# Preamble of a fused convolution and LoRA kernel: taps and bias loaded as whole rows, three unread products, the first pair's merges and chunks in another order, B's high part stored by itself

## The chip, the cores and the metric

One core of a Trainium2 chip runs the kernel. The metric is the device time of one execution in microseconds; less is better.

## The reference, cut to what matters

x has 64 samples of 64 channels by 1024 positions. First comes a grouped convolution along the positions (4 groups, 9 taps, padding 4), plus a context per sample and channel and a bias:

```
out = conv(x, weight, groups=4) + (c @ c_weight.T)[:, :, None] + bias[None, :, None]
```

Its result, seen as 8 batches of 512 rows by 1024, goes through a dense layer with LoRA: a kernel W of 1024 by 1024 and a bias, a pair A, B per batch (gate, 8 by 16, mixes 16 of them; rank 32) and a shared pair:

```
y @ W + bias + (y @ A_eff[b].T) @ B_eff[b].T + (y @ A_s.T) @ B_s.T
```

and x is added. Everything is float32.

## The kernel before, in words

**Tiling.** A batch b has 8 samples; a half h of it holds two of the four groups, and each group t of a half is one tile of 128 rows, for which TensorE computes `main[t]`. A pair of tiles (b, h) is a *unit*; the sixteen units run one after the other. For speed in float32, each operand is split into a high part (`x_hi`, `y_hi`, `w_hi`) and a low part, the rest (`x_lo`, ...), and three products of the parts are summed. ScalarE makes high parts, GpSimd (and VectorE for some of the first) the low ones by a subtraction; VectorE takes convolution results out of PSUM (`y_add`) and transposes them (`y_stage`). From the second batch on the convolution has a fast form with three products per tile (`fast`, L890 to L892), which also needs differences of x: `xd` and, in place, `x_tr` (`x_diff`, L649 and L653), turned into `xd_hi`, `x_hi` (L505, L507) and `xd_lo`, `x_lo` (L358, L360).

**The preamble.** Before the loop everything is prepared and the first pair of tiles is computed beside it. The taps `w_pad` are spread out to `z_all` (L599), transposed by TensorE (L827), and split into `t_hi`, `t_lo`. The context is `cond` times `cond_w` plus a bias column `cb_col`; TensorE brings the 64 words `cbias` to the partitions with a product by a selection matrix `sel` (L834), and multiplies at L842. `gmix` is gate, spread by TensorE (L955). With it, TensorE mixes A (`mix_a`, L914; VectorE turns the result in `a_turn`, L687, into `a_eff`) and B (`mix_b`, L927; `b_turn`, L692, into `be_raw`). The shared pair is merged into W: `merge(m)` (L902) multiplies half m of B_s A_s, `w_add(m)` (L683, VectorE) adds it to `w_raw`, `w_high(k)` (ScalarE, L511) and `w_low(k)` (GpSimd, L383) split chunk k of 8. `chunk(k)` then multiplies the first pair by chunk k: eight products by `w_hi`, then four by `w_lo`. The first four convolution tiles are `convolve(0, 0, i)` and `y_tile(0, 0, i)`; the order of everything is written out by hand for each engine, and each engine works its own list strictly in order, with semaphores between them.

The first half of x is transposed by VectorE in four pieces (L612), then split (L470, L676 on VectorE for t = 0, L334 on GpSimd for t = 1); the second half of x follows in the same way.

**B for the later batches.** `be_raw` is split into `be_hi` (L550) and `be_lo` (L398); the first batch's rows go to `b_cur` with six transfers (L266, semaphore `b_first`), and all of both parts to HBM, `b_scratch`, with eight (L274, semaphore `be_out`), after both parts are complete. The memory of `be_hi` is used again by `xd_hi` and `xd_lo`: so `x_high(2, ...)` on ScalarE waits for `b_first` and for all of `be_out`. SyncE (SP) issues nearly all transfers, in the order of its list; ScalarE's queue issues the taps, `cond_nat`, `cw_nat` and `cbias`.

**The steady part.** From the second unit on, `unit(b, h)` on TensorE has 48 products of 512 columns per tile with W (L936: 8 chunks, 3 products of parts, 2 halves of the columns), the product with A (L949), the low rank part (L941) and two fast convolutions for the next unit. Output goes from `res` to HBM by SyncE.

Of the kernel before, what the change touches and what calls it, by code (L numbers as in the profile page):

```python
# [5 lines left out]
F32 = mybir.dt.float32  # L6
F32R = mybir.dt.float32r
ALU = mybir.AluOpType
ACT = mybir.ActivationFunctionType
# [41 lines left out]
def adaln_ffn(nc, x, x_rows, cond, cond_bias, conv_w, cond_w, gate, kern, bias,  # L51
# [10 lines left out]
    with ctx:  # L62
# [9 lines left out]
        def early(*specs):  # L72
# [32 lines left out]
        (w_pad, cond_nat, cw_nat, cond_t, cw_rep, cbias, cb_col, sel, gate_nat, gate_rep, diag) = early(  # L105
            ("w_pad", [C, CG, PAD + TAPS + PAD], F32), ("cond_nat", [NS, CD], F32), ("cw_nat", [C, CD], F32),
            ("cond_t", [CD, NS], F32), ("cw_rep", [P, G, J, CG], F32), ("cbias", [CG, G], F32), ("cb_col", [P, G], F32), ("sel", [CG, J, CG], F32),
# [14 lines left out]
        ident_ready, halo_zero, pad_zero = sem("ident_ready"), sem("halo_zero"), sem("pad_zero")  # L122
# [7 lines left out]
        ctx_mm, ctx_done, sel_done = sem("ctx_mm"), sem("ctx_done"), sem("sel_done")  # L130
# [6 lines left out]
        be_hid, be_lod, be_out, b_first = sem("be_hid"), sem("be_lod"), sem("be_out"), sem("b_first")  # L137
# [78 lines left out]
        def _(sp):  # L216
            load_first(sp, 0)
# [106 lines left out]
        def _(pool):  # L324
# [4 lines left out]
            pool.wait_ge(ident_ready, 2)  # L329
            nc.gpsimd.tensor_copy(sel[:, :, :], ident[0:CG, 0:CG].unsqueeze(1).broadcast_to([CG, J, CG])).then_inc(sel_done, 1)  # L330
# [116 lines left out]
        def _(act):  # L447
            act.dma_start(w_pad[:, :, PAD:PAD + TAPS], conv_w).then_inc(cw_in, 16)
            act.dma_start(cond_nat[:, :], cond).then_inc(cond_in, 16)
            act.dma_start(cw_nat[:, :], cond_w).then_inc(cond_in, 16)  # L450
            with nc.allow_non_contiguous_dma(reason="sixty-four words"):
                act.dma_start(cbias[:, :], cond_bias.rearrange("(g c) -> c g", g=G)).then_inc(cbias_in, 16)
# [9 lines left out]
            nc.scalar.activation(cb_col[:, :], rank[:, 128:128 + G], ACT.Copy).then_inc(cond_cp, 1)  # L462
# [10 lines left out]
            act.wait_ge(tlo_done, 2)  # L473
            nc.scalar.activation(t01_raw[:, :, :, :].rearrange("p g s c -> p s g c"),
                                 main[0][:, 512:1024].rearrange("p (s g c) -> p s g c", s=J, g=G), ACT.Copy).then_inc(t01_copied, 1)
# [8 lines left out]
            nc.scalar.activation(bias_hi[:, :], bias_nat[:, :], ACT.Copy).then_inc(bias_split, 1)  # L484

# [47 lines left out]
            w_high(3)  # L533
# [52 lines left out]
        def _(dve):  # L586
            nc.vector.memset(w_pad[:, :, 0:PAD], 0.0).then_inc(pad_zero, 1)
            nc.vector.memset(w_pad[:, :, PAD + TAPS:], 0.0).then_inc(pad_zero, 1)
# [7 lines left out]
            dve.wait_ge(pad_zero, 2)  # L596
            dve.wait_ge(cw_in, 16)
            wide = PAD + TAPS + PAD
# [108 lines left out]
            dve.wait_ge(bs_in, 48)  # L707
            nc.vector.transpose(bs_t[0:STACK, :].rearrange("r (p o) -> r o p", p=R), bs_rep[0:STACK, :, :]).then_inc(bs_turned, 1)
# [395 lines left out]
```

## Time and profile before

| | |
|---|---|
| median of 3 runs | 509.15 us (508.51 to 509.65) |
| the profiled execution | 507.94 us |
| its span in the trace | 506.1 us |
| TensorE busy (matmuls) | 488.4 us, 96% |
| weight loads of TensorE | 403.1 us, 80% |
| VectorE, ScalarE, GpSimd busy | 332.9, 166.7, 272.7 us |
| chain that ended last: TensorE, DMA, VectorE | 90%, 3%, 2% |
| transfers | 65.04 MB, mean 129 GB/s |

Busy time of TensorE is the time in which a matmul is under way; matmuls overlap, so it doesn't say how fast they go. Times below are microseconds from the start of the span. A row of a timeline gives the start, the duration, the engine (PE is TensorE, PEld its weight loads, DVE VectorE, ACT ScalarE, POOL GpSimd, SPq and ACTq the queues that issue transfers), the line, the operation, its output and inputs, shapes, the number of instructions merged, and in brackets how long the engine had been idle and what ended that.

### The profile page before, as it was taken

How to read it: one execution, taken by the hardware profiler on the slowest of the kernel's cores; microseconds unless marked ns; L12 is line 12 of the kernel's file. 1: busy time of each engine (PE TensorE's matmuls, PEld its weight loads, DVE VectorE, ACT ScalarE, POOL GpSimd, SP SyncE). 2: the span in 40 equal slices, each digit the busy share in tenths (PEclk: the TensorE clock that was granted, in tenths of full speed). 3: DMA queues.
4: the chain of work that ended last, by engine and by line, in shares of the span. 5: the costliest groups of instructions: out<-in, count | busy, mean ns of one | idle time of the engine just before them, and what ended most of it. 6: DMA issues, size and time to landing. Idle time of an engine off the chain costs nothing.

```text
span 506.1 us, 6740 instructions
## 1 busy us (share of the span) xinstructions
PE 488.4 (96%) x2394; PEld 403.1 (80%) x2394; DVE 332.9 (66%) x384; ACT 166.7 (33%) x210; POOL 272.7 (54%) x157
## 2 busy tenths in 40 slices
PE   2999998999999999999999999999999999999995
PEld 2777886788888888888888888888888888888884
DVE  4786585996938497575939397575948488473411
ACT  2566313341525123331524224331433234331100
POOL 0789943792847439272756529282665619382200
PEclk9999999899999999999999999999999999999998
DMA  8953526751724326241634326241633313241303
GB/s 216 416 217 138 188 69 172 243 199 67 240 94 114 83 70 239 51 128 41 230 102 111 86 52 241 57 124 55 214 117 100 97 29 83 66 122 63 99 27 83
DMA packets 19029, 65.04 MB, mean 129 GB/s; under 512 B 2728, under 2 KB 3368, under 8 KB 18376
## 3 DMA queue, kind: packets, MB, share of 16 engines
q1 hardware_dynamic: 17736, 64.77, 41.3%
q10 hardware_dynamic: 1280, 0.10, 0.2%
q8 instruction: 8, 0.13, 0.1%
q14 instruction: 5, 0.04, 0.0%
HBM read 45.59 MB, written 18.87 MB: 127 GB/s over the span
## 4 chain that ended last, share of the span: by engine, by line
PE 90%; DMA 3%; DVE 2%; POOL 1%; ACT 1%; SPq 1%; issue 0%; ACTq 0%; DVEq 0%
PE main L936 65%; PE rank L949 5%; PE main L941 3%; PE conv L890 3%; PE conv L892 3%; PE conv L891 3%; PE conv L866 2%; DMA cbias<-in_fside_S 2%; PE main L914 1%; PE spare L892 1%; PE spare L891 1%; PE spare L890 1%; SPq L274 1%; DMA b_scratch<-be_lo 1%; PE conv L927 1%; POOL x_lo L360 1%
## 5 line engine op out<-in xcount | busy, mean ns | idle before, releaser
L936 PE MATMUL main<-w_hi,y_hi 128*128 128x512 f32 x512 | 160.1, 391 | 0.0
L936 PE MATMUL main<-w_hi,y_lo 128*128 128x512 f32 x512 | 159.0, 389 | 0.0
L936 PE MATMUL main<-w_lo,y_hi 128*128 128x512 f32 x512 | 158.2, 390 | 0.0
L936 PEld LDWEIGHTS main<-w_lo,y_hi 128*128 128x128 f32 x512 | 96.4, 188 | 20.6
L378 POOL TENSOR_TENSOR y_lo<-y_stage,y_hi 128x512 fp32r<-128x512 f32 x56 | 94.0, 1701 | 34.0 <-ACT y_hi L494 34.0
L936 PEld LDWEIGHTS main<-w_hi,y_lo 128*128 128x128 f32 x512 | 96.1, 188 | 20.3
L936 PEld LDWEIGHTS main<-w_hi,y_hi 128*128 128x128 f32 x512 | 95.3, 188 | 19.4
L358 POOL TENSOR_TENSOR xd_lo<-xd,xd_hi 128x512 fp32r<-128x512 f32 x28 | 39.3, 1404 | 104.2 <-ACT xd_hi L505 104.2
L360 POOL TENSOR_TENSOR x_lo<-x_tr,x_hi 128x1024 fp32r<-128x1024 f32 x28 | 82.6, 2948 | 16.5 <-ACT x_hi L507 16.5
L507 ACT ACTIVATE x_hi<-x_tr 128x1024 fp32r<-128x1024 f32 x28 | 57.7, 2061 | 30.0 <-DVE x_tr L653 30.0
L494 ACT ACTIVATE y_hi<-y_stage 128x512 fp32r<-128x512 f32 x56 | 35.5, 634 | 90.2 <-DVE y_stage L671 90.2
L671 DVE STREAM_TRANSPOSE y_stage<-y_add 128x512 f32<-128x512 f32 x56 | 62.9, 1163 | 0.0
L761 DVE TENSOR_TENSOR ax_sum<-rank,ax_sum 32x256 f32<-32x256 f32 x16 | 6.6, 412 | 71.4 <-ACT ax_sum L518 71.4
L769 DVE TENSOR_TENSOR res<-main,res 128x1024 f32<-128x1024 f32 x31 | 37.5, 1210 | 22.9 <-PE main L941 22.9
L505 ACT ACTIVATE xd_hi<-xd 128x512 fp32r<-128x512 f32 x28 | 17.8, 634 | 99.0 <-DVE xd L649 87.7
L653 DVE TENSOR_TENSOR x_tr<-x_tr 128x512 f32<-128x512 f32 x28 | 46.1, 1646 | 1.0
L649 DVE TENSOR_TENSOR xd<-x_tr 128x512 f32<-128x512 f32 x28 | 39.9, 1423 | 4.4 <-POOL xd_lo L358 4.4
L612 DVE STREAM_TRANSPOSE x_tr<-x_in 128x512 f32<-128x512 f32 (+1 forms) x64 | 39.3, 678 | 1.8 <-DMA x_in<-in_x_rows 1.6
L662 DVE TENSOR_TENSOR y_add<-conv,ctx_all 128x512 f32<-128x512 f32 x28 | 19.1, 684 | 22.8 <-PE conv L892 22.8
L949 PE MATMUL rank<-y_hi,a_cur 128*64 128x256 f32 x128 | 29.9, 277 | 0.0
L949 PE MATMUL rank<-y_lo,a_cur 128*64 128x256 f32 x128 | 29.9, 277 | 0.0
L518 ACT ACTIVATE ax_sum<-rank 32x256 f32<-32x256 f32 x16 | 6.0, 373 | 60.4 <-PE rank L949 60.4
(105 smaller groups left out, 489.1 us busy)
## 6 DMA issues: line engine op xcount, KB each, us to landing
res<-in_x SPq DMA_DIRECT2D x32, 512.0 KB
out<-res SPq DMA_DIRECT2D x31, 512.0 KB
x_in<-in_x_rows SPq DMA_DIRECT2D x7, 2048.0 KB, 12.8
w_raw<-in_L_ffn_kernel SPq DMA_DIRECT2D x4, 1024.0 KB, 17.8
b_cur<-b_scratch SPq DMA_DIRECT2D x21, 128.0 KB, 3.1
la<-in_L_ffn_lora_A SPq DMA_DIRECT2D x4, 512.0 KB, 8.1
lb<-in_L_ffn_lora_B SPq DMA_DIRECT2D x1, 2048.0 KB, 8.1
x_in<-in_x_rows SPq DMA_DIRECT2D x1, 1048.0 KB, 7.7
```

The costliest lines, as they stand in the source:

```text
L358: nc.gpsimd.tensor_tensor(xd_lo[:, t], xd[:, :, :], xd_hi[:, t].bitcast(F32), ALU.subtract).then_inc(xlo_done, 1)
L360: nc.gpsimd.tensor_tensor(x_lo[:, t, :, 0:NP], x_raw(2 * h + t, 0, NP), x_hi[:, t, :, 0:NP].bitcast(F32), ALU.subtract).then_inc(xlo_done, 1)
L378: nc.gpsimd.tensor_tensor(y_parity(y_lo, h, t, e), y_staged(e), y_parity(y_hi, h, t, e).bitcast(F32), ALU.subtract).then_inc(ylo_done, 1)
L494: nc.scalar.activation(y_parity(y_hi, h, t, e), y_staged(e), ACT.Copy).then_inc(yhi_done, 1)
L507: nc.scalar.activation(x_hi[:, t, :, 0:NP], x_raw(2 * h + t, 0, NP), ACT.Copy).then_inc(xhi_done, 1)
L612: nc.vector.transpose(x_tr[:, m0:m1, :, :].rearrange("p m n g -> p m (n g)"), blocks).then_inc(xt_done, 1)
L649: nc.vector.tensor_tensor(xd[:, :, :], x_block(0, 1, g), x_block(1, 0, g), ALU.subtract).then_inc(xd_done, 1)
L653: nc.vector.tensor_tensor(x_block(0, 0, g), x_block(0, 0, g), x_block(1, 0, g), ALU.subtract).then_inc(xd_done, 1)
L671: nc.vector.transpose(y_stage[:, e, :].rearrange("p (a l n c) -> p a n l c", a=2, l=2, n=SB), y_add[:, e, :].rearrange("p (a m n) -> p a n ...
L769: nc.vector.tensor_tensor(res[:, g, :], main[g % 2][:, :], res[:, g, :], ALU.add).then_inc(main_free, 1)
L936: mm(main[t][:, n * 512:(n + 1) * 512], lhs, rhs[:, k, n * 512:(n + 1) * 512], start=k == 0 and first, stop=False)
L949: last = mm(rank[0:2 * R, 0:2 * P], lhs, y[h][:, :, k, :], start=k == 0 and y is y_hi, stop=k == KC - 1 and y is y_lo)
```

## The change

Six things change, all in the preamble.

1. The taps are loaded as 64 whole rows (`w_nat`, 576 bytes each) and VectorE copies them into `w_pad`, in place of a transfer of 1024 pieces of 36 bytes.
2. The bias of the context is loaded as one row of 64 words, first on SyncE's queue. GpSimd repeats it (`bias_rep`), and four products of one row by one word (`ones`) bring it to `spare`; ScalarE copies it to `cb_col`. The matrix `sel` and its product are gone.
3. `fill(n)`: n products of `ident` with itself, 512 columns, into `main[1]`, which nobody reads. Two before the taps' transposes, one before the gate's product.
4. The first pair's work stands in another order: on TensorE `mix_a(2)` and `mix_a(3)` move forward, merges 4 to 11 move behind the chunks one step further; VectorE turns A before the second `y_tile`, makes `gmix` before it turns `bs_t`, and takes `w_add(6)` and `w_add(7)` after `y_tile(0, 0, 2)`; ScalarE and GpSimd exchange some `w_high`/`w_low` and `y`/`x` operations; the copy of `t01_raw` moves behind the split of the shared pair.
5. The four stores of `be_hi` are issued when `be_hi` is complete, with a semaphore of their own, `be_out[0]`; those of `be_lo` follow with `be_out[1]`.
6. `x_high(2, ...)` waits for `be_out[0]` and for the last `be_lod`, not for the stores of `be_lo`.

```
 sync:
+            sp.dma_start(cbias[:, :], cond_bias.rearrange("(a c) -> a c", a=1)).then_inc(cbias_in, 16)
             load_first(sp, 0)
...
-            sp.wait_ge(be_hid, RQ)
-            sp.wait_ge(be_lod, RQ)
-            for i, part in enumerate((be_hi, be_lo)):
+            for i, (part, split) in enumerate(((be_hi, be_hid), (be_lo, be_lod))):
+                sp.wait_ge(split, RQ)
                 for oh in range(2):
                     for bq in range(2):
...
-                                     part[row:row + R, :, :].bitcast(F32)).then_inc(be_out, 16)
+                                     part[row:row + R, :, :].bitcast(F32)).then_inc(be_out[i], 16)
             sp.wait_ge(b_first, 96)
-            sp.wait_ge(be_out, 128)
+            sp.wait_ge(be_out[0], 64)
+            sp.wait_ge(be_out[1], 64)
 gpsimd:
-            pool.wait_ge(ident_ready, 2)
-            nc.gpsimd.tensor_copy(sel[:, :, :], ident[0:CG, 0:CG].unsqueeze(1).broadcast_to([CG, J, CG])).then_inc(sel_done, 1)
+            nc.gpsimd.memset(ones[:, :], 1.0).then_inc(biasrep_done, 1)
+            pool.wait_ge(cbias_in, 16)
+            nc.gpsimd.tensor_copy(bias_rep[:, :, :, :], cbias[:, :].rearrange("a (g c) -> a g c", g=G)
+                                  .unsqueeze(2).broadcast_to([1, G, J, CG])).then_inc(biasrep_done, 1)
...
             w_low(2)
             x_first_low(1)
+            y_low_first(2)
             w_low(3)
-            y_low_first(2)
+            y_low_first(3)
             x_low_second(0)
-            y_low_first(3)
             w_low(4)
 scalar:
-            act.dma_start(w_pad[:, :, PAD:PAD + TAPS], conv_w).then_inc(cw_in, 16)
+            act.dma_start(w_nat[:, :], conv_w.rearrange("o c k -> o (c k)")).then_inc(cw_in, 16)
...
-                act.dma_start(cbias[:, :], cond_bias.rearrange("(g c) -> c g", g=G)).then_inc(cbias_in, 16)
...
-            nc.scalar.activation(cb_col[:, :], rank[:, 128:128 + G], ACT.Copy).then_inc(cond_cp, 1)
+            act.wait_ge(bias_mm, 1)
+            nc.scalar.activation(cb_col[:, :], spare[:, 64:64 + G], ACT.Copy).then_inc(cond_cp, 1)
...
-                    act.wait_ge(be_out, 128)
+                    act.wait_ge(be_out[0], 64)
+                    act.wait_ge(be_lod, RQ)
...
             x_first_high(1)
-            w_high(3)
             act.wait_ge(a_done, RQ)
...
             y_high_first(0, 2, FIRST)
+            w_high(3)
             x_high_second(0)
+            y_high_first(0, 3, FIRST)
             w_high(4)
-            y_high_first(0, 3, FIRST)
+            x_high_second(1)
             w_high(5)
-            x_high_second(1)
 vector:
+            nc.vector.tensor_copy(w_pad[:, :, PAD:PAD + TAPS], w_nat[:, :].rearrange("o (c k) -> o c k", k=TAPS)).then_inc(pad_done, 1)
+            dve.wait_ge(pad_done, 3)
...
             y_tile(0, 0, 0, FIRST, first=True)
+            a_turn(0)
             y_tile(0, 0, 1, FIRST, first=True)
-            a_turn(0)
+            a_turn(1)
...
-            a_turn(1)
+            a_turn(2)
             w_add(0)
             w_add(1)
-            a_turn(2)
+            a_turn(3)
             w_add(2)
             w_add(3)
-            a_turn(3)
...
+            x_first_low(1)
+            y_tile(0, 0, 2, FIRST, first=True)
             w_add(6)
             w_add(7)
-            x_first_low(1)
-            y_tile(0, 0, 2, FIRST, first=True)
-            w_add(8)
-            w_add(9)
             y_tile(0, 0, 3, FIRST, first=True)
-            w_add(10)
-            w_add(11)
+            for m in range(8, 12):
+                w_add(m)
 tensor:
+            def fill(n):
+                for _ in range(n):
+                    mm(main[1][:, 0:512], ident[:, :], ident[:, :].unsqueeze(1).broadcast_to([P, 4, P]), start=True, stop=True)
             pe.wait_ge(ident_ready, 2)
+            fill(2)
...
+            pe.wait_ge(biasrep_done, 2)
+            for g in range(G):
+                last = mm(spare[:, 64 + g:65 + g], bias_rep[:, g, :, :].rearrange("a j c -> a (j c)"), ones[:, :], start=True, stop=True)
+            last.then_inc(bias_mm, 1)
...
+            fill(1)
             pe.wait_ge(gate_cp, 1)
...
             mix_a(0)
             mix_a(1)
+            mix_a(2)
             merge(0)
             merge(1)
-            mix_a(2)
+            mix_a(3)
             merge(2)
             merge(3)
-            mix_a(3)
-            merge(4)
-            merge(5)
...
             chunk(0)
+            merge(4)
+            merge(5)
+            chunk(1)
+            convolve(0, 0, 2, FIRST, first=True)
             merge(6)
             merge(7)
-            chunk(1)
-            convolve(0, 0, 2, FIRST, first=True)
+            chunk(2)
+            convolve(0, 0, 3, FIRST, first=True)
             merge(8)
             merge(9)
-            chunk(2)
-            convolve(0, 0, 3, FIRST, first=True)
+            chunk(3)
             merge(10)
             merge(11)
-            chunk(3)
             mix_b(0)
```

## Rows read from the trace of the kernel before

**Rows 1.** Windows of 100 to 500 us, their sum by engine.

```profile
sum 400.00, PE 400.00 PEld 333.09 DVE 261.15 ACT 124.55 POOL 208.18; mean PE 44.44 PEld 37.01 DVE 29.02 ACT 13.84 POOL 23.13
```

**Rows 2.** Timeline of the first 25 us, all engines.

```profile
5.67 1.22 DVE L599 COPY z_all<-w_pad 64x2048 f32<-64x2048 f32 x1 [3.78 <-DMA w_pad<-in_L_cond_weight]
...
7.04 1.94 PE L827 MATMUL main<-ident,z_all 64*128 64x64 f32 x16 [7.04 <-DVE z_all L599]
...
8.54 2.56 DVE L612 STREAM_TRANSPOSE x_tr<-x_in 128x544 f32<-128x544 f32 x4 [1.64 <-DMA x_in<-in_x_rows]
...
12.93 2.10 ACT L470 ACTIVATE x_hi<-x_tr 128x528 fp32r<-128x528 f32 x2
12.94 1.94 PE L842 MATMUL rank<-cond_t,cw_rep 128*128 128x64 f32 x8 [0.89 <-ACT cb_col L462]
14.06 1.08 DVE L676 TENSOR_TENSOR x_lo<-x_tr,x_hi 128x528 fp32r<-128x528 f32 x1 [1.79 <-ACT x_hi L470]
...
15.39 2.08 DVE L708 STREAM_TRANSPOSE bs_t<-bs_rep 96x1024 f32<-96x1024 f32 x1
...
18.37 0.69 DVE L631 TENSOR_TENSOR y_add<-conv,ctx_all 128x512 f32<-128x512 f32 x1 [0.85 <-PE conv L866]
...
24.82 0.68 DVE L683 TENSOR_TENSOR w_raw<-rank,w_raw 128x512 f32<-128x512 f32 x1
```

**Rows 3.** Chain that ended last, before 100 us: start, duration, what.

```profile
15.40 4.44 PE conv L866 x24
...
44.90 1.87 PE conv L927 x8
...
47.44 2.74 PE main L936 x12
...
55.47 2.84 PE conv L866 x24
...
77.79 4.84 DMA b_scratch<-be_lo
```

**Rows 4.** Waits of TensorE before 100 us: total, times, longest.

```profile
PE conv L890 <- POOL x_lo L360: 2.5, 1, 2.5
```

**Rows 5.** Windows, 90 to 100 us: engines, granted clock, DMA share, GB/s.

```profile
90.00:100.00 10.00, 10.00 (x38) 8.02 (x37) 9.76 (x9) 3.98 (x4) 6.86 (x5) 0.83 0.77 253
```

**Rows 6.** Timeline of 78 to 97 us, all engines.

```profile
78.30 1.07 DVE L649 TENSOR_TENSOR xd<-x_tr 128x512 f32<-128x512 f32 x1
...
82.79 0.63 ACT L505 ACTIVATE xd_hi<-xd 128x512 fp32r<-128x512 f32 x1 [11.38 <-DMA b_scratch<-be_lo]
...
85.43 3.28 POOL L360 TENSOR_TENSOR x_lo<-x_tr,x_hi 128x1024 fp32r<-128x1024 f32 x1 [0.63 <-ACT x_hi L507]
...
93.27 2.96 POOL L360 TENSOR_TENSOR x_lo<-x_tr,x_hi 128x1024 fp32r<-128x1024 f32 x1 [3.14 <-ACT x_hi L507]
```

**Rows 7.** DMA issues before 100 us: queue, count, KB each, us to landing.

```profile
x_in<-in_x_rows SPq DMA_DIRECT2D x1, 1048.0 KB, 7.7
...
w_pad<-in_L_cond_weight ACTq DMA_DIRECT2D x1, 36.0 KB, 4.8
...
cw_nat<-in_L_cond_c_weight ACTq DMA_DIRECT2D x1, 32.0 KB, 8.0
```

**Rows 8.** DMA issues between 71.5 and 72 us.

```profile
b_scratch<-be_hi SPq DMA_DIRECT2D x1, 256.0 KB, 2.7
```

**Rows 9.** GpSimd's groups of instructions, 32.9 to 46 us: busy, mean ns.

```profile
L383 POOL TENSOR_TENSOR w_lo<-w_raw,w_hi 128x1024 fp32r<-128x1024 f32 x3 | 7.3, 2418 | 1.3 <-ACT w_hi L511 1.3
L352 POOL TENSOR_TENSOR x_lo<-x_tr,x_hi 128x1040 fp32r<-128x1040 f32 x1 | 3.0, 3005 | 0.5 <-ACT x_hi L525 0.5
L366 POOL TENSOR_TENSOR y_lo<-y_stage,y_hi 128x512 fp32r<-128x512 f32 x2 | 2.6, 1306 | 0.0
```

**Rows 10.** Timeline of 34 to 46 us, VectorE and GpSimd.

```profile
34.19 2.08 DVE L676 TENSOR_TENSOR x_lo<-x_tr,x_hi 128x512 fp32r<-128x512 f32 x1
...
45.99 4.76 POOL L383 TENSOR_TENSOR w_lo<-w_raw,w_hi 128x1024 fp32r<-128x1024 f32 x2
```

More of the change, by code:

```diff
@@ L104, in adaln_ffn @@
         y_add, y_stage = sb("y_add", [P, 2, 512]), sb("y_stage", [P, 2, 512])
-        (w_pad, cond_nat, cw_nat, cond_t, cw_rep, cbias, cb_col, sel, gate_nat, gate_rep, diag) = early(
+        (w_pad, cond_nat, cw_nat, cond_t, cw_rep, cbias, cb_col, bias_rep, ones, w_nat, gate_nat, gate_rep, diag) = early(
             ("w_pad", [C, CG, PAD + TAPS + PAD], F32), ("cond_nat", [NS, CD], F32), ("cw_nat", [C, CD], F32),
-            ("cond_t", [CD, NS], F32), ("cw_rep", [P, G, J, CG], F32), ("cbias", [CG, G], F32), ("cb_col", [P, G], F32), ("sel", [CG, J, CG], F32),
+            ("cond_t", [CD, NS], F32), ("cw_rep", [P, G, J, CG], F32), ("cbias", [1, C], F32), ("cb_col", [P, G], F32),
+            ("bias_rep", [1, G, J, CG], F32), ("ones", [1, 1], F32), ("w_nat", [C, CG * TAPS], F32),
             ("gate_nat", [NB, NL], F32),
@@ L120, in adaln_ffn @@
         rank = ps("rank", [P, 512])
-        ident_ready, halo_zero, pad_zero = sem("ident_ready"), sem("halo_zero"), sem("pad_zero")
+        ident_ready, halo_zero, pad_done = sem("ident_ready"), sem("halo_zero"), sem("pad_done")
         cw_in, cond_in, cbias_in, gate_in = sem("cw_in"), sem("cond_in"), sem("cbias_in"), sem("gate_in")
@@ L129, in adaln_ffn @@
         cond_tr, cond_cp, cwrep_done = sem("cond_tr"), sem("cond_cp"), sem("cwrep_done")
-        ctx_mm, ctx_done, sel_done = sem("ctx_mm"), sem("ctx_done"), sem("sel_done")
+        ctx_mm, ctx_done, bias_mm, biasrep_done = sem("ctx_mm"), sem("ctx_done"), sem("bias_mm"), sem("biasrep_done")
         gate_cp, gate_tr, diag_done, gmix_done = sem("gate_cp"), sem("gate_tr"), sem("diag_done"), sem("gmix_done")
@@ L136, in adaln_ffn @@
         a_mm, a_done, b_mm, b_turned = sem("a_mm"), sem("a_done"), sem("b_mm"), sem("b_turned")
-        be_hid, be_lod, be_out, b_first = sem("be_hid"), sem("be_lod"), sem("be_out"), sem("b_first")
+        be_hid, be_lod, b_first = sem("be_hid"), sem("be_lod"), sem("b_first")
+        be_out = [sem(f"be_out{i}") for i in range(2)]
         x0_hi, x0_lo, x0_pool, y0_lo = sem("x0_hi"), sem("x0_lo"), sem("x0_pool"), sem("y0_lo")
@@ L447, in _ @@
         def _(act):
-            act.dma_start(w_pad[:, :, PAD:PAD + TAPS], conv_w).then_inc(cw_in, 16)
+            act.dma_start(w_nat[:, :], conv_w.rearrange("o c k -> o (c k)")).then_inc(cw_in, 16)
             act.dma_start(cond_nat[:, :], cond).then_inc(cond_in, 16)
             act.dma_start(cw_nat[:, :], cond_w).then_inc(cond_in, 16)
-            with nc.allow_non_contiguous_dma(reason="sixty-four words"):
-                act.dma_start(cbias[:, :], cond_bias.rearrange("(g c) -> c g", g=G)).then_inc(cbias_in, 16)
             for w in range(2):
@@ L484, in _ @@
             nc.scalar.activation(bias_hi[:, :], bias_nat[:, :], ACT.Copy).then_inc(bias_split, 1)
+            act.wait_ge(tlo_done, 2)
+            nc.scalar.activation(t01_raw[:, :, :, :].rearrange("p g s c -> p s g c"),
+                                 main[0][:, 512:1024].rearrange("p (s g c) -> p s g c", s=J, g=G), ACT.Copy).then_inc(t01_copied, 1)
             def y_high_first(u, i, order):
@@ L586, in _ @@
         def _(dve):
-            nc.vector.memset(w_pad[:, :, 0:PAD], 0.0).then_inc(pad_zero, 1)
-            nc.vector.memset(w_pad[:, :, PAD + TAPS:], 0.0).then_inc(pad_zero, 1)
+            nc.vector.memset(w_pad[:, :, 0:PAD], 0.0).then_inc(pad_done, 1)
+            nc.vector.memset(w_pad[:, :, PAD + TAPS:], 0.0).then_inc(pad_done, 1)
             nc.vector.memset(x_in[:, :, 0:HALO], 0.0).then_inc(halo_zero, 1)
@@ L706, in _ @@
                                     cb_col[:, :].unsqueeze(2).broadcast_to([P, G, NS]), ALU.add).then_inc(ctx_done, 1)
-            dve.wait_ge(bs_in, 48)
-            nc.vector.transpose(bs_t[0:STACK, :].rearrange("r (p o) -> r o p", p=R), bs_rep[0:STACK, :, :]).then_inc(bs_turned, 1)
             dve.wait_ge(diag_done, 1)
@@ L712, in _ @@
                                     spare[:, 0:NB].unsqueeze(2).broadcast_to([P, NB, R8]), ALU.mult).then_inc(gmix_done, 1)
+            dve.wait_ge(bs_in, 48)
+            nc.vector.transpose(bs_t[0:STACK, :].rearrange("r (p o) -> r o p", p=R), bs_rep[0:STACK, :, :]).then_inc(bs_turned, 1)
             dve.wait_ge(ctx_done, 1)
             y_tile(0, 0, 0, FIRST, first=True)
+            a_turn(0)
             y_tile(0, 0, 1, FIRST, first=True)
-            a_turn(0)
+            a_turn(1)
             dve.wait_ge(t01_copied, 1)
@@ L830, in _ @@
                 last.then_inc(t_tr, 1)
-            pe.wait_ge(cbias_in, 16)
-            pe.wait_ge(sel_done, 1)
-            mm(rank[:, 128:128 + G], sel[:, :, :].rearrange("a j c -> a (j c)"), cbias[:, :],
-               start=True, stop=True)
             pe.wait_ge(cond_in, 32)
```

4 lines of the change are left out of this document (removed).

## The prediction

> **What bounds the kernel now.** I read the stretches of the span first. Between 100 and 500 us TensorE is busy for all 400 us at the full granted clock [rows 1], and the table of waits has no wait of TensorE after 88.8 us. So four fifths of the kernel is a TensorE stream that the change leaves alone: what it saves or loses before 100 us arrives at the end unchanged, and nothing else counts.
>
> Then the waits and the timeline before 100 us. TensorE starts at 7.04 us, when the spread-out taps are there [rows 2]; it is held twice between 9 and 13 us; its first convolutions (24 products) take 4.44 us, where the same work later takes 2.84 us [rows 3]: they start at the 1.2 GHz level, and the spacing of the products halves near 18.2 us, 5.2 us after the stream of work without a pause began at 12.94 us [rows 2]. (The granted-clock column says 1.00 here; the durations say otherwise, and I go by them.) From 15.3 to 86.1 us TensorE hardly pauses. Then it waits 2.5 us for GpSimd's x_lo [rows 4], and afterwards the granted clock of 90 to 100 us is 0.83 on average [rows 5]: the clock fell to 1.2 GHz behind the pause, which cost 0.17 x 10 = 1.7 us more.
>
> The chain of waits says why x_lo was late: the last store of B's low part, issued at 77.79 us, lands 4.84 us later [rows 3], and ScalarE's xd_hi sat 11.38 us until that [rows 6], since its buffer lies where be_hi lay. The data of xd_hi, VectorE's first difference, was there at 79.37 us.
>
> **Part by part: the taps and the bias.** The taps now come as 64 rows of 576 bytes instead of 1024 pieces of 36 bytes. Before: issue at 0.75 us, landing 4.8 us later [rows 7]. The quickest landing of a larger transfer in this trace took 2.7 us (256 KB) [rows 8]; I take that: 3.45 us. VectorE's new copy of 64x144 isn't in the trace; between nothing and the 1.22 us of z_all [rows 2], near 0.2 us by its size. z_all then ends at 4.95 us, TensorE starts at 5.05 (2.0 earlier) and ends its 16 transposes at 7.0. With no gain in the landing all of this stays at 7.0 and 9.0.
>
> The context's weights landed 8.0 us after their issue, at 10.15 us [rows 7], behind the 1024 pieces on the same queue. I take them as there by 7.0 us (2.7 us after issue would be 4.9; at worst 10.15 as before). The bias as one row on SyncE's queue replaces 64 single words on ScalarE's. It pushes the load of x by one issue, about 0.7 us. x landed 7.7 us after 0.74 [rows 7]; less the load of the small pieces, plus the 0.7 us, it lies between 6.7 and 9.2 us; I take 7.6. The chunk transposes [rows 2] then run to 10.15 us.
>
> The four new bias products on TensorE are like the context's eight entries (four products, 1.94 us, [rows 2]), and before there was one product of 0.58 us. They end at 7.0 + 0.5 (transposes of the context) + 1.94 = 9.45 us; ScalarE turns over cond_t and cw_rep beside them, copies the bias by 9.7 and starts x_hi at 10.2 us (before 12.93 [rows 2]). Context products 9.75 to about 11.1 us. **The fills**: two of them lie in time when TensorE has nothing else (1.5 to 3.4 us) and cost nothing; the third is an fp32 product of 512 columns, 1.87/4 = 0.47 us by the four of L927 [rows 3], twice that at 1.2 GHz, and it is on the path. The gate product 0.3 us, so the convolutions begin at 11.9 us. TensorE works nearly without a pause from 5.05 us; if the clock rises as long after this as before (5.2 us), it is up at 10.3 and the convolutions take 2.84 us: until 14.75 instead of 19.8 us.
>
> At the small pieces the trace shows 4.8 us for 36 KB and 2.7 us for 256 KB [rows 7, 8]. The Trainium skill (DMA: Bandwidth & Descriptors, Specifications) wants at least 512 bytes a transfer for the full rate, which 576 bytes meets and 36 doesn't; the trace agrees in direction. By the rule alone the gain would be the whole excess, the 2.1 us that I took; by the row, without it, nothing between 0 and 2.1 is excluded.
>
> **VectorE sets the next date.** x_lo (1.08 us, [rows 2]) ends at 12.5, context and gmix by 13.3, and bs_t of 2.08 us at 15.4: y_add starts there instead of at 18.37 us [rows 2]. From it to the end of the second sum of W were 7.1 us before, 0.3 of that idle; the new order puts one more turn of A (0.7 us) in: 7.6 us, so 23.0 us instead of 25.5 [rows 2]. The turn of A that now stands ahead of the second y_tile needs mix_a(0), which TensorE ends at 14.75 + 1.9 = 16.65, and VectorE is ready for it at 17.2: just no wait. W's first low part is done at 26.55 us, 2.5 earlier.
>
> **The interleaving gives most of it back.** TensorE now computes chunk 0 (2.74 us, [rows 3]) before merges 4 and 5, and must wait for that low part: chunk 0 and merges end near 27.9 us. VectorE's sums 4 and 5, the chunk transposes, x_hi and x_lo follow one another, and the third convolution ends at 34.2 us instead of 36.8, with about 2 us of waits of TensorE around it. w_add 6 and 7 are now behind y_tile 2, so w_hi(3) comes at 37.4 us (before 35.1), and GpSimd, on which y_low(2) now precedes w_low(3), stands still for some 2.9 us in three pieces until 41.5. Left to do there: y_low 1.3 and x_low 3.0 us [rows 9]; w_low(4) starts at 45.8 us, where it was 45.99 [rows 10]. From there GpSimd works without a pause until 60 us in both. TensorE has its chunk 4 at 49.1 instead of 50.2 us and keeps 1.0 us of the 5 it had won.
>
> In that stretch VectorE's second x_lo took 2.08 us [rows 10] where the first, of nearly the same shape, took 1.08 [rows 2]; GpSimd was working each time from some point on, in the second throughout. The Trainium skill (SBUF — State Buffer, Who interferes with whom) says that an operation of VectorE with two inputs in SBUF and one of GpSimd that reads SBUF hold one port in turn, and the second is blocked. By the rule a free port would give 1.08 us and end the third convolution 1 us sooner; by the schedule above GpSimd has w_low(2) there, and I keep 2.08.
>
> **B's high part by itself.** The four stores of be_hi are issued right behind the six pieces of b_cur, near 62.8 us, instead of at 71.7; the low ones stay. xd_hi waits for the high ones (landed by about 70) and the last be_lo (71.67), both past long before its data. xd was done at 79.37 [rows 6], 1.0 less for the front: 78.4. Second difference to 79.5, x_hi 2.0 to 81.6, x_lo 3.3 to 84.95. TensorE arrives at 86.1 - 1.0 = 85.1: the wait of 2.5 us is gone, and with it the fall of the clock, 1.7 us. Next late is the second x_lo: it ended 7.5 us behind the first (88.71 and 96.23, [rows 6]), so at 92.45; TensorE, which reached it at 96.86, now does at 96.86 - 1.0 - 2.5 - 1.7 = 91.66. New wait 0.8 us. SyncE's residual loads and first output store move 3 us forward with the stores, and their waits are SyncE's own. The early 1 MB of stores may delay the load of x for the second pair (landed 68.0, used at 73.4): 4 us of cover.
>
> **Sum**: front 1.0 + wait 2.5 + clock 1.7 - new wait 0.8 = 4.4 us. The profiled execution took 507.94 us (span 506.1 and 1.8 around it): 503.5. The median of the runs shown is 509.15, 1.2 higher; I forecast on it: 504.8 us.
>
> **Rivals.**
> - Late clock. If the short transposes don't bring the clock up and it stays at 1.2 GHz through the convolutions, these run from 13.1 to 17.6 us, mix_a(0) ends at 19.5, and VectorE is held behind the turn of A 2.3 us: front -1.3, time 507.1. For it: at 7 to 9 and 11 to 15 us such work didn't raise it. Against it: then it paused.
> - GpSimd isn't the bound. If the order leaves it no gaps (y_stage of tile 2 earlier, or the port free), the 2.5 us of the W chain arrive whole, or more with x landing at 6.7: front 2.5 to 3.5, time near 502.8.
> - The store was not the last wait, and xd_hi is held by something else (b_first, be_lod): front only, 508.1. The trace speaks against it: be_lod is at 71.67, b_first before 67.
> - Slower. Landings come no sooner (context's weights at 10.15) and the clock stays down: bias, context, fill and gate put the convolutions at 16.3 to 21.5 us, mix_a(0) to 23.5, and VectorE, blocked behind the turn of A in its queue, is 6.3 us later than forecast: 511.1 us. It decides from the point where that turn starts after 22.6 us instead of 17.2. With landings late but the clock as before, 5.0 us later, it ends at 509.8, inside what is no change.
>
> **Numbers.** Forecast 0.42 (503.2 to 506.2); late clock 0.20; GpSimd not the bound 0.18; store not the last wait 0.06; no change 0.07; slower 0.07. Range 502.3 to 508.0 us takes the first three and their bounds. About 0.2% (1.0 us) is what a measurement of this kernel can tell. Faster: 0.42 + 0.20 + 0.18 and part of the store case, 0.83; same 0.10; slower 0.07.
>
> **What would show it.** z_all ending near 5 us; TensorE's convolutions from 11.9 us with products at full speed; y_add at 15.4; w_low(4) of GpSimd near 45.8, with gaps before; no wait at the first fast convolution near 85 us, a granted clock of 1.0 for 85 to 95 us, and one wait under 1 us near 92. Wrong if TensorE's waits around the third convolution make the clock fall (up to 1.7 us more), if w_low(4) is more than 1 us from its date, or if the second x_lo doesn't follow the first by 7.5 us.

## The result: 0.5% slower, where 0.9% faster was forecast

The changed kernel takes 510.67 us (median of 14 runs, 509.03 to 512.49); the kernel before takes 508.18 us (median of 14, 507.07 to 509.67). The ratio is 1.0054, with a 95% interval of 1.0040 to 1.0067. The forecast was 504.8 us; it stood on 509.15 us for the kernel before, the median of three runs, which is 1.0 us above that of fourteen. The profiled execution of the changed kernel took 510.24 us, its span 508.4 us, 2.3 more than before.

The part after 100 us has not changed, as [rows 1] answer to. Windows of the changed kernel: us, then busy time of PE, PEld, DVE, ACT, POOL, the granted clock, the DMA share (the mean busy share of the 16 DMA engines), GB/s:

```profile
0.00:9.00 9.00, 5.14 (x20) 2.46 (x20) 2.19 (x8) 2.38 (x3) 1.34 (x8) 1.00 0.73 190
9.00:19.00 10.00, 7.50 (x26) 5.78 (x27) 5.99 (x10) 5.25 (x10) 2.89 (x3) 0.51 1.03 336
...
90.00:100.00 10.00, 9.71 (x43) 7.68 (x42) 9.48 (x9) 4.67 (x6) 6.88 (x4) 1.00 0.87 239
100.00:500.00 400.00, 400.00 (x1867) 333.00 (x1866) 264.25 (x292) 125.12 (x154) 211.43 (x115) 1.00 0.37 110
```

TensorE is busy for all 400 us from 100 to 500, so the loss is ahead of that. The clock of 90 to 100 us is 1.00 where it was 0.83 [rows 5]: the end of the preamble went as forecast. The clock of 9 to 19 us is 0.51, close to the 1.2 GHz level for the whole stretch. The waits of TensorE in the changed kernel (total, times, longest) say the same:

```profile
PE rank L842 <- DMA cw_nat<-in_L_cond_c_weight: 4.5, 1, 4.5
PE main L946 <- POOL w_lo L388: 1.6, 2, 1.2
...
PE conv L876 <- DVE x_lo L682: 0.9, 1, 0.9
PE conv L876 <- ACT x_hi L474: 0.8, 1, 0.8
PE conv L900 <- POOL x_lo L365: 0.3, 1, 0.3
```

The wait of 2.5 us for x_lo [rows 4] has shrunk to 0.3. The wait for the context's weights is 4.5 us; before, TensorE came to that place 2.3 us later and waited 2.1 us for the bias words and 0.9 for ScalarE's copy of them. New are 3.3 us in four waits around the third convolution and the chunks. Of the chain that ended last, to 55 us (start, duration, what):

```profile
1.97 9.22 DMA cw_nat<-in_L_cond_c_weight
...
11.71 1.80 PE spare L847 x8
...
13.76 1.97 PE rank L852 x8
15.73 1.81 PE main L830 x2
17.55 0.52 PE spare L966 x2
18.07 3.71 PE conv L876 x24
21.78 5.49 PE main L924 x90
...
28.00 1.25 DVE w_raw L689 x2
...
44.15 1.45 PE conv L876 x12
...
48.37 1.29 POOL y_lo L371
49.67 2.98 POOL x_lo L357
52.65 2.35 POOL w_lo L388
```

The load of the weights lasts 9.2 us from its issue; the bias products (1.80), the context (1.97) and the unread fill (1.81 us) follow. The convolutions run from 18.1 to 21.8 us; the forecast was 11.9 to 14.75, and before it was 15.4 to 19.84 [rows 3]. The start is 2.7 us later than before: 1.8 are the unread fill, 1.2 the four bias products in place of one (1.80 for 0.58), 0.2 the later landing (the weights at 11.19, before the bias words at 11.02); 0.6 come back, since less of ScalarE's copying stands between. The same stretch in the timeline of the changed kernel, rows that answer to [rows 2]:

```profile
3.01 0.23 DVE L602 COPY w_pad<-w_nat 64x144 f32<-64x144 f32 x1 [1.11 <-DMA w_nat<-in_L_cond_weight]
3.27 1.22 DVE L605 COPY z_all<-w_pad 64x2048 f32<-64x2048 f32 x1
...
5.26 1.43 PE L837 MATMUL main<-ident,z_all 64*128 64x64 f32 x16
...
10.60 2.56 DVE L618 STREAM_TRANSPOSE x_tr<-x_in 128x544 f32<-128x544 f32 x4 [6.11 <-DMA x_in<-in_x_rows]
...
20.45 0.69 DVE L637 TENSOR_TENSOR y_add<-conv,ctx_all 128x512 f32<-128x512 f32 x1
...
23.77 0.72 DVE L693 STREAM_TRANSPOSE a_eff<-main 128x512 f32<-128x512 f32 x1 [1.39 <-PE main L924]
...
28.58 0.67 DVE L689 TENSOR_TENSOR w_raw<-rank,w_raw 128x512 f32<-128x512 f32 x1
```

The taps are early, z_all ends at 4.49 us (before 6.89), and the transposes run faster (1.43 us for the same 16 products that took 1.94 [rows 2]). Then nothing more is there to compute: x and the context's weights are still on their way. The turn of A starts at 23.77 us, behind TensorE: the rival that ended slower named that sign, after 22.6 us instead of 17.2, and 511.1 us.

GpSimd has w_low(4) at 52.62 us, 6.6 later than before [rows 10]. At the end of the preamble, in the timeline of ScalarE and GpSimd (the answer to [rows 6]), the stores are gone as a cause:

```profile
85.56 0.64 ACT L510 ACTIVATE xd_hi<-xd 128x512 fp32r<-128x512 f32 x1 [8.07 <-DVE xd L655]
...
88.75 2.97 POOL L365 TENSOR_TENSOR x_lo<-x_tr,x_hi 128x1024 fp32r<-128x1024 f32 x1 [1.02 <-ACT x_hi L512]
...
96.27 2.96 POOL L365 TENSOR_TENSOR x_lo<-x_tr,x_hi 128x1024 fp32r<-128x1024 f32 x1 [3.12 <-ACT x_hi L512]
```

ScalarE's xd_hi waits for VectorE's xd alone. The second x_lo starts 7.52 us behind the first.

### The profile page after: what moved, and what is told of

The parts are those of the page before. It is cut to its first block, busy times and chain, and to the rows that moved or that the text cites. A ratio compares the mean times of both kernels' runs of the same rounds, so it can differ in the third digit from the quotient of the medians.

```text
span 508.4 us, 6762 instructions
## 1 busy us (share of the span) xinstructions
PE 493.3 (97%) x2406; PEld 404.2 (79%) x2406; DVE 333.8 (66%) x385; ACT 167.0 (33%) x210; POOL 273.2 (54%) x158
## 4 chain that ended last, share of the span: by engine, by line
PE 88%; DVE 4%; POOL 2%; DMA 2%; ACT 2%; issue 1%; ACTq 0%; DVEq 0%
PE main L946 63%; PE rank L959 5%; PE main L951 3%; PE conv L900 3%; PE conv L901 2%; PE conv L902 2%; PE conv L876 2%; DMA cw_nat<-in_L_cond_c_weight 2%; PE spare L902 1%; PE spare L901 1%; PE spare L900 1%; DVE x_tr L618 1%; PE main L924 1%; POOL w_lo L388 1%; ACT x_hi L512 1%
## 5 line engine op out<-in xcount | busy, mean ns | idle before, releaser
L946 PEld LDWEIGHTS main<-w_hi,y_lo 128*128 128x128 f32 x512 | 96.1, 188 | 20.3
```

Source lines behind the costliest of these rows:

```text
L946: mm(main[t][:, n * 512:(n + 1) * 512], lhs, rhs[:, k, n * 512:(n + 1) * 512], start=k == 0 and first, stop=False)
```

## The experiments

Twelve kernels, in three series, each with its own runs of the kernel before (medians 508.01, 508.15 and 508.23 us). A ratio is to the kernel before. Where the new loads are kept with the old order, `gmix` still stands ahead of the turn of `bs_t`, since in the new layout they share memory in that order.

### First series: each part by itself

**store_alone**: the kernel before with items 5 and 6.

```
-            sp.wait_ge(be_hid, RQ)
-            sp.wait_ge(be_lod, RQ)
-            for i, part in enumerate((be_hi, be_lo)):
+            for i, (part, split) in enumerate(((be_hi, be_hid), (be_lo, be_lod))):
+                sp.wait_ge(split, RQ)
...
-                    act.wait_ge(be_out, 128)
+                    act.wait_ge(be_out[0], 64)
+                    act.wait_ge(be_lod, RQ)
```

> The kernel before with only the stores of be_hi split off and the shorter wait of x_high (items 5 and 6 of the change). Theory: in the changed kernel this part worked and gave back 3.9 us of a front that was 6.3 us late (there the first fast convolution no longer waits and the clock doesn't fall). Then alone it takes 3.5 to 4 us off the time of the kernel before (its wait of 2.5 us, 1.7 us of slow clock, less a small wait at the second x_lo), ratio near 0.992. Rival: it gained in the changed kernel only because the late front moved everything else; then alone it gives under 1 us.

Measured: 504.51 us, ratio 0.9929 (0.9916 to 0.9942), 3.6 us less. xd_hi starts at 80.44 us (82.79 in [rows 6]), TensorE waits 0.3 us for x_lo in place of 2.5, and the granted clock of 90 to 100 us is 1.00. In total the store part is worth what was forecast, 2.5 + 1.7 - 0.8 = 3.4 us; on the 1.7 us of slow clock in this sum see "The store" below.

**order_alone**: the kernel before with item 4.

```
             mix_a(0)
             mix_a(1)
+            mix_a(2)
             merge(0)
             merge(1)
-            mix_a(2)
+            mix_a(3)
...
-            merge(4)
-            merge(5)
             chunk(0)
+            merge(4)
+            merge(5)
+            chunk(1)
```

> The kernel before with only the new order of merges, chunks, turns and splits (item 4). Theory: the order costs 2.5 to 3 us, whatever stands before it, since the second W sums wait for merges 4 and 5 behind chunk 0 and GpSimd has gaps until w_low(4); w_low(4) starts near 48.5 to 49 us instead of 46.0, and the time is 2 to 3 us above the kernel before. Rival: the order is harmless by itself and only loses when the front is late, since mix_a(0) then holds VectorE behind the turn of A; then under 1 us here.

Measured: 512.33 us, ratio 1.0085 (1.0072 to 1.0098). This is the largest single effect of the series. Windows of its profile:

```profile
37.00:39.00 2.00, 1.11 (x9) 0.91 (x9) 1.29 (x1) 1.70 (x4) 2.00 (x2) 0.99 0.84 328
39.00:41.00 2.00, 2.00 (x6) 1.54 (x5) 1.77 (x3) 0.00 (x0) 0.66 (x1) 0.50 1.07 459
```

TensorE is busy for 1.11 of 2 us, waiting 0.8 and 0.9 us for the split halves of x, and behind that the clock falls to 0.50. w_low(4) starts at 52.31 us, 6.3 later than before.

**loads_alone**: the kernel before with items 1 and 2.

```
-            act.dma_start(w_pad[:, :, PAD:PAD + TAPS], conv_w).then_inc(cw_in, 16)
+            act.dma_start(w_nat[:, :], conv_w.rearrange("o c k -> o (c k)")).then_inc(cw_in, 16)
```

> The kernel before with the taps and the context's bias as whole rows (items 1 and 2), no unread products, the old order except that gmix is made before bs_t is turned. Theory: the taps are there 2 us sooner, but the context's weights and the first x land 1 and 2 us later, and the four bias products stand behind them: convolutions start 0.5 to 1 us later than 15.3 us, time +0.5 to +1.5 us. Rival: the late landings came from the rest of the change; then x lands at 8.5 us as before and the convolutions start sooner, time -1 us or less.

Measured: 507.02 us, ratio 0.9982 (0.9972 to 0.9992), 0.9 us less. Not through an earlier front: in the profile the convolutions start at 16.4 us, 1.1 us later than before, for the weights landed 9.4 us after their issue. What the profile shows of a gain comes at the other end. Its wait of TensorE:

```profile
PE conv L894 <- POOL x_lo L364: 2.1, 2, 1.6
```

And its window of 90 to 100 us:

```profile
90.00:100.00 10.00, 9.43 (x42) 7.37 (x41) 9.76 (x9) 3.96 (x4) 6.86 (x5) 1.00 0.85 229
```

The wait ends when the store has landed, as in the kernel before; TensorE comes later, waits 1.6 and then 0.5 us, and the clock does not fall. The last store is issued 1.2 us later than before (79.00 against 77.79) and lands 0.3 us later.

**fills_alone**: the kernel before with item 3.

```
             pe.wait_ge(ident_ready, 2)
+            fill(2)
...
+            fill(1)
             pe.wait_ge(gate_cp, 1)
```

> The kernel before with the three unread products only (item 3). Theory: one such product is 0.9 us at 2.4 GHz and 1.8 us at 1.2 GHz; the first two (until 5.3 us) are hidden before the taps' transposes at 7.0 us; the third costs its own 0.9 to 1.8 us ahead of the first convolutions. If the two keep the clock up until the convolutions (unbroken work from 7 us nearly), these gain up to 1.6 us back: time between -0.5 and +1.5 us. Rival: the clock falls again before the convolutions, as in the changed kernel, and nothing comes back: +1.5 us or more.

Measured: 507.49 us, ratio 0.9997 (0.9988 to 1.0006): nothing. In the profile the third fill takes 1.81 us and the convolutions start at 17.1 us, 1.7 later than before, and again it is hidden at the late store, which lands at 82.79 us (before 82.63): waits of 1.5 and 0.6 us in place of 2.5, the clock of 90 to 100 us at 1.00.

### Second series: one part taken back, and the order in halves

**order_back**: the changed kernel with the old order (item 4 undone).

> The changed kernel with the order of before (gmix still ahead of bs_t): loads, unread products and split stores stay. Theory: the order costs some 4 us in the changed kernel (w_low(4) 6.6 us late, of which the convolutions' late start is 2); without it w_low(4) starts near 48 us, the late stores don't bind, and the time is near 506 us, 4 to 5 us below the changed kernel and under the kernel before. Rival: the late loads and the third unread product are what makes it slow; then this is still at 509 us or more.

Measured: 506.69 us, ratio 0.9969 (0.9959 to 0.9979), 0.85% below the changed kernel, the same as order_alone had added. (Its profiled execution, 505.12 us, was the lowest of its nine, so the profile shows it about 1.6 us too good.) It is 2.2 us above store_alone by the medians, and the profiles don't show where: the fill stands in the chain with 1.81 us, from 14.75 to 16.56, and the convolutions start at 17.1 instead of 15.4 us, but they take 3.71 us here and 5.27 in store_alone's profile, so that they end at 20.80 and 20.69 us, and both spans are 503.3 us.

**no_fills**: the changed kernel with item 3 undone.

> The changed kernel without its three unread products. Theory: the third costs 1.8 us on the path at the lower clock, but the clock then rises later among the convolutions, so that 0.5 to 1.5 us come off the changed kernel's time. Rival: the products pay for themselves; then the time is that of the changed kernel within 0.3 us.

Measured: 509.28 us, ratio 1.0017 (1.0008 to 1.0026), 0.37% or 1.9 us below the changed kernel. The convolutions start at 15.3 us, as before the change, and the kernel is still slower than before, although it has the store's gain. From its chain:

```profile
15.34 4.37 PE conv L870 x24
19.70 5.47 PE main L918 x86
...
38.13 0.73 PE conv L870 x4
...
39.72 3.95 PE main L940 x12
```

Three mixes of A (5.47 us) stand ahead of the first merge, where there were two (3.71 us in the chain of the kernel before). Behind the waits around 38 us the products of chunk 2 take 3.95 us instead of 2.74 [rows 3]: the clock is down here too.

**order_mix**: the kernel before with the first half of item 4 (mixes of A forward, turns of A, `gmix` before `bs_t`, the copy of `t01_raw` later).

> The kernel before with one half of the new order: mix_a(2) ahead of the first merges, mix_a(3) ahead of the next, the turns of A ahead of y_tile 1 and of the W sums, gmix before bs_t, the copy of t01 later. Merges 4 to 11 and GpSimd's order as before. Theory: it makes the first W sum 1.9 us later and nothing else; this moves w_low(4) by 1.9 us, of which the wait for the late store of B hides most: time between -1 and +1 us. Rival: this half is what costs order_alone its 4.3 us.

Measured: 509.23 us, ratio 1.0025 (1.0012 to 1.0038). w_low(0) starts at 29.01 us, 2.35 later than before (26.66). Its chain has the three mixes as a row of 5.48 us, 1.8 more than before, and its convolutions ended 0.5 us later. w_low(4) starts at 47.31, 1.3 later. Here the late store hides nothing: its last part is issued at 79.07 us, 1.3 later than before, and lands at 83.95, 1.3 later too.

**order_chunks**: the kernel before with the other half (merges 4 to 11 behind the chunks, `w_add` 6 and 7 behind `y_tile` 2, the exchanges on ScalarE and GpSimd).

```
 gpsimd:
-            w_low(3)
             y_low_first(2)
-            x_low_second(0)
+            w_low(3)
             y_low_first(3)
+            x_low_second(0)
```

> The kernel before with the other half of the new order: merges 4 to 11 behind the chunks, w_add 6 and 7 behind y_tile 2, y_low and x_low ahead of w_low 3 and 4. Theory: GpSimd gets gaps of 3 us and TensorE waits at chunk 0, at the third convolution and at chunk 4; w_low(4) starts 4.5 us later than 46.0 and the time is 1.5 to 3.5 us above the kernel before. Rival: the waits vanish when mix_a isn't moved, and the time is that of before.

Measured: 511.37 us, ratio 1.0060 (1.0046 to 1.0074). Its chain says where:

```profile
32.12 0.25 PE spare L900
...
33.06 0.68 DVE w_raw L683
33.75 1.19 DVE x_tr L612 x2
...
34.96 1.10 ACT x_hi L470
...
36.08 2.09 DVE x_lo L676
...
38.21 0.74 PE conv L864 x4
...
42.16 1.45 PE conv L864 x12
...
46.35 1.28 POOL y_lo L366
47.63 3.02 POOL x_lo L352
50.66 2.35 POOL w_lo L383
```

The merge that now comes behind chunk 0 holds VectorE's sum, behind which the last transposes of x, x_hi and x_lo are queued: x_lo starts at 36.08 us instead of 34.19 [rows 10]. And GpSimd now takes x_low_second (3.0 us) behind y_low(3), which waits for the fourth convolution; in the order before it was done in that wait. w_low(4) starts at 50.62 us, 4.6 later. The rows divide this: the fourth convolution ends at 43.61 us, 1.9 later than before (41.70), which is the first cause; from there to w_low(4) are 7.0 us, before 4.3, which is the second. No run tests them one by one. The two halves of the order, 0.25% and 0.60%, add up to order_alone's 0.85%.

### Third series: combinations with the old order

**store_loads**: items 1, 2, 5 and 6, no fills. **store_taps**: the same, with the bias as before the change.

> Split stores (items 5, 6) and whole rows of taps and bias (items 1, 2) on the kernel before; old order except gmix ahead of bs_t, no unread products. Theory: alone the loads gave -1.0 us only because a later front shortens TensorE's wait for the late store, so that the clock doesn't fall; with the stores split nothing hides the front, and the loads cost 0.5 to 1 us against store_alone: ratio to before 0.994 to 0.995. Rival: the loads really save 1 us; then ratio 0.991.

> As store_loads, but with the bias as in the kernel before (64 words on ScalarE's queue, product with sel): only the taps are whole rows. Theory: one product of 0.6 us stands in place of four of 1.8 us ahead of the context's, and x's load isn't pushed, but the first convolutions wait for the context's weights and x as before: store_alone within 0.5 us, and up to 1 us below store_loads. Rival: the taps' 2 us come through; then 1.5 us or more below store_alone.

Measured: 504.45 us, ratio 0.9930 (0.9914 to 0.9945), and 504.50 us, 0.9927 (0.9911 to 0.9943). Beside store_alone's 0.9929 the loads are worth nothing, and neither route of the bias is better. In store_loads the weights land at 10.0 us and the convolutions start at 15.0 (before 15.3).

**shared_late**: store_loads with two loads of A ahead of the shared pair's six loads.

```
+            for q in range(2):
+                sp.dma_start(la[:, q, :], la_v[:, q, :]).then_inc(la_in[q], 16)
             for q in range(3):
                 load_shared(sp, q)
```

> As store_loads, but SyncE issues the first two loads of A ahead of the six loads of the shared pair (32 partitions each). Theory: between 7 and 12 us the transfers move only some 220 GB/s while all engines are busy, because loads into 32 partitions are under way; they hold x and the context's weights. With them later, x lands 1 to 2 us sooner, the context's weights as well, and the time is up to 1 us below store_loads. Rival: x lands when it did, or the shared pair becomes the late one (bs_t waits) and the time rises by up to 2 us.

Measured: 503.83 us, ratio 0.9919 (0.9904 to 0.9934), 0.6 us below store_loads, with intervals that overlap. The front does move. Issues of the two transfers in this kernel (KB, us to landing), which took 7.7 and 8.0 us before [rows 7]:

```profile
x_in<-in_x_rows SPq DMA_DIRECT2D x1, 1048.0 KB, 6.7
...
cw_nat<-in_L_cond_c_weight ACTq DMA_DIRECT2D x1, 32.0 KB, 6.9
```

The convolutions start at 13.8 us, 1.2 us sooner than in store_loads, but take 4.61 us, where the same work takes 2.84 later [rows 3]; w_low(4) starts at 44.74 (46.22 in store_loads), and then a mix of B waits 0.7 us for its load, which is now later.

**bias_behind_x**: store_loads with the bias row issued behind x and the gate on SyncE.

> As store_loads, but the bias row is issued behind x and the gate on SyncE's queue instead of ahead of x. Theory: x is issued 0.4 us sooner and lands 0.4 us sooner; the bias is there long before its use; time equal to store_loads or up to 0.4 us less. Rival: the transfer ahead of x is what made it land 2 us later in the changed kernel; then over 1 us less.

Measured: 503.28 us, ratio 0.9910 (0.9892 to 0.9927). It is the fastest of all and beats both kernels, store_loads by 1.2 us, but again with overlapping intervals. The weights landed 7.3 us after issue, the convolutions start at 14.3 us. That the bias's place causes this isn't shown: x and the weights landed between 7.7 and 9.4 us, and between 7.3 and 9.4, in kernels whose loads hardly differ.

## Why the prediction was wrong

**The sum.** Four runs lead from the kernel before to the changed one: the store -0.71% (store_alone), the loads 0 (store_loads), the fills +0.39% (order_back), the order +0.85% (the changed kernel). That such steps add up to the measured 0.54% is no check. A check is that another pair of kernels gives each of the two losses again: 0.37% for the fills (the changed kernel against no_fills), 0.85% for the order (order_alone). The forecast had the store at -3.4 us and all the rest at -1.0 us. The store was -3.6 us; the rest, +2.5 + 3.6 = +6.1 us, reversed the sign.

**The step that failed: "the convolutions begin at 11.9 us".** They began at 18.1, 6.2 us later. By the chain, 4.1 us of this are the end of the bias products (13.5 against 9.45), set by the landing of the context's weights; 1.3 the fill, 0.6 the context's products (1.97 against 1.35), 0.2 the gate's. In the forecast's terms:
- "I take them as there by 7.0 us" (the context's weights): they were there at 11.2 us, outside even the bound of 10.15. The forecast counted the 1024 pieces as what held them. Removing the pieces brought the taps themselves 2.6 us forward (2.2 us to landing instead of 4.8 [rows 7]) but not what was queued beside and behind them. x landed 9.3 us after its issue, at 10.5 us, where 7.6 was taken and 9.2 was the bound. What held both was not the pieces; between 7 and 12 us the DMA share is 1.05 in the changed kernel, and when six other loads were issued later (shared_late), both landed 1.1 us sooner than in store_loads. Why they took 9.3 and 9.2 us here, and 7.8 and 8.0 in store_loads with the same loads, no run shows. The Trainium skill (DMA: Bandwidth & Descriptors, Queues, rings and completion order) says that each DMA engine takes its queues in turn; the trace fits this in that a small load on ScalarE's queue is as slow as SyncE's large one, 9.2 beside 9.3 us, but no run tests it.
- "TensorE works nearly without a pause from 5.05 us; ... it is up at 10.3": true until 6.7 us. Then came the pause of 4.5 us, and the clock fell (0.51 for 9 to 19 us), so bias, context, fill and gate all ran at 1.2 GHz. In loads_alone, which has no fills, the bias products take 1.80 and the context's 1.97 us as well: for these the fills at the start changed nothing. The Trainium skill (TensorE: Matmul & The Clock Gate, HAM oscillation — how this bites in real kernels) describes the same: TensorE goes back to the low clock in a wait for a DMA between short bursts. The fills won 0.5 us for the transposes and nothing behind the wait.
- "0.47 us by the four of L927, twice that at 1.2 GHz" (the fill): 1.81 us. That was the wrong row. The products of L927 fill 64 output partitions each, the fill 128, and the two fills at the start, 3.78 us, are as slow as the third. By the third's 1.81 us at 1.2 GHz, a fill at 2.4 GHz would be about 0.9 us, an estimate, and not 0.47. The Trainium skill (TensorE: Matmul & The Clock Gate, Why this matters for your kernels) says that products into separate groups of output partitions run at the same time, which would halve L927's price against the fill's; the durations fit, but no run here tests it.
- The bias products (1.80 us against 1.94), the copy of the taps (0.23 against 0.2) and the landing of the taps (2.2 against 2.7, so that z_all ended at 4.49 instead of 4.95) were right.

**The second failing step: "VectorE sets the next date".** With an early start TensorE's three mixes of A would have ended before VectorE was ready (14.75 + 5.5 = 20.3 us, with W's first sum at 21.7), and the extra 1.9 us ahead of merges 0 and 1 would have cost nothing. With the late start TensorE sets the date: 21.78 + 5.49 (mixes) + 0.7 (merges) + 1.3 (two sums) = 29.3, measured 29.25 us, forecast 23.0. order_mix shows the price at the old start: 2.35 us on w_low(0), 0.5 of it from slower convolutions, and 0.25% in the end. What the same order would do with convolutions from 11.9 us wasn't tried: no kernel here got a start below 13.8 us.

**The interleaving, forecast as a loss, was sized right.** From the second sum of W to w_low(4) the forecast had 22.8 us; measured are 23.4 (29.25 to 52.62); before it was 20.5. What was missed is that the loss comes whole when the front brings nothing. The forecast said of the clock that TensorE's waits around the third convolution might make it fall, up to 1.7 us more: this happened in order_alone and no_fills (0.50 behind 39 us), not in the profiles of the changed kernel and order_chunks, whose waits are as long. It may have happened in other executions of the changed kernel. Eight of its fourteen have a mean granted clock of 0.984, 0.985 or 0.995 and took 510.6 to 512.5 us; the other six, with the profiled one among them, have 0.987 to 0.989 or 0.997 and took 509.0 to 510.5. Which stretch was slow in the eight no trace shows, and no kernel here was made to test it.

**The store was right in its signs and in its total, but not in every term.** xd_hi follows xd; the first fast convolution has no wait; the second has 0.3 us (forecast 0.8); the clock is 1.00; the second x_lo follows by 7.52 us (7.5). The front was 6.1 us late at the convolution of [rows 3]'s 55.47 (now 61.55); at the second fast convolution 2.0 were left (99.29 against 97.25 in the chain of the kernel before; the forecast took 96.86 for this date, and with 97.25 its new wait would be 0.4), and the span is 2.3 longer. The 1.7 us of slow clock are a term of one profile. Of the 59 runs of the kernel before that stand beside the experiments, 32 have a mean granted clock of 0.998 or 0.999, too high for a loss of 1.7 us (it would be 0.997 or less), and their median is 507.9 us, against 508.3 for the other 27. So most runs have no such fall, and the two medians are only 0.45 us apart. That the total came out at 3.6 us is in part luck, and what makes up the rest of it stays open.

**What the forecast had no step for.** The late store also hid lateness in two kernels. Its landing fixed the time of the first fast convolution, and a front 1.2 us late at 55.47 us [rows 3] (56.68 in loads_alone, 56.62 in fills_alone) only shortened TensorE's wait, since the landing moved by 0.3 and 0.2 us. It is not a rule: in order_mix the front is as late (56.78), the landing moves by 1.3 us, and so does the time. Nor is the shorter wait shown to be why the clock didn't fall in those two profiles: in order_alone and order_chunks TensorE waits 2.7 and 2.6 us at the same place, until 94.8 and 92.9 us, and the clock stays up too. From order_alone:

```profile
PE conv L888 <- POOL x_lo L360: 2.7, 1, 2.7
...
90.00:100.00 10.00, 7.29 (x33) 5.64 (x32) 7.90 (x8) 5.65 (x7) 6.23 (x4) 1.00 0.83 200
```

With the store split, the fills cost 0.39%, and alone nothing. So the parts don't add up from runs of each alone (-0.71 - 0.18 - 0.03 + 0.85 = -0.07%, measured +0.54%). The runs beside the other parts (0.37 to 0.39% for the fills, 0.85% for the order, nothing for the loads) say what each costs in the changed kernel.

**The chances.** The rival that ended slower got 0.07, since the trace of before has landings of 2.7 us for 256 KB [rows 8]. That landing is from 71.5 us, where the DMA share of the next 3 us is 0.62 and 135 GB/s move; between 7 and 12 us the share of the kernel before is 1.05 ([rows 7]: 8.0 us for 32 KB). The nearest row in size was not the nearest in load, and with this choice a start 6 us too early stood in the forecast.

## What to carry to other kernels

A landing time is taken from the stretch in which the transfer runs, by what else moves then, not from a quiet one. Before an order is changed to fit an earlier start, make sure that the start is early: with the old start the new order costs 0.85% here. And where a late event may hide part of the work ahead of it, try each part beside the removal of that event as well as alone.

## What the runs showed of the hardware

- The load of x (1 MB) took 6.7 to 9.4 us and that of 32 KB of weights 6.9 to 9.4 us, with almost the same list of transfers. The DMA share from 7 to 12 us was 1.01 to 1.06 in all; what was moved from 7 to 12 us was 216 GB/s in store_loads, 240 before, and 290 in shared_late, where the six loads of the shared pair came later.
- An fp32 product of 128 rows by 512 columns into 128 partitions took 1.81 us in the stretch at 1.2 GHz; four of L927's, into 64 partitions each, took 1.87 us at 2.4 GHz, 0.47 us each (the profile has two rows for each product).
- After a wait of 2.5 us the granted clock fell (0.66 for 90 to 95 us of the kernel before; order_mix the same), after 2.7 us (order_alone) and 2.6 us (order_chunks) it stayed at 1.00, and after 1.6 and 0.5 us (loads_alone) and 1.5 and 0.6 us (fills_alone) as well. Around the third convolution two waits of 0.8 and 0.9 us were followed by a fall in two profiles and not in two others. So the length of the wait alone doesn't tell these cases apart.
- The granted-clock column said 1.00 for 0 to 9 us of the changed kernel, while two fp32 products took 3.78 us; their durations, not the column, show the 1.2 GHz level. The same four bias products took 1.80 us where the column says 0.50 (the changed kernel) and where it says 1.00 (loads_alone).
- The same 24 products of the first convolutions took 3.71 us (the changed kernel, order_back) to 5.37 us (store_taps) from one profile to the next, so a single profile's start of them doesn't tell when they end.
